# Group 0 of an embedding loop: shift and normalise moved one block on, and two weight low parts formed earlier

## The reference

```python
h = tok(x, emb0..emb3, proj0..proj3)                  # adaptive embedding: a row of one of 4 tables, times its projection
h = h + attn(layernorm(h), w1, v1, w2, conv, A, B, C, D)
h = h + ffn(layernorm(h), shared experts, 8 routed experts, top 2 by a hash of the position)
...
x1 = x @ w1_w.T + w1_b
x_conv = _silu(_depthwise_conv(x1, conv_w))           # 3 taps
x_ssm = _ssm(x_conv, A, B_ssm, C_ssm, D_ssm)          # a linear recurrence over the position
v = _silu(x @ v1_w.T + v1_b)
return x_ssm * v @ w2_w.T + w2_b
```

## Time and profile before

| | us |
|---|---|
| median of 3 runs | 439.96 (439.94 to 440.4) |
| the profiled execution, its own time | 440.18 |
| its span in the profile | 438.3 |
| PE busy | 399.5 (91%) |
| DVE, ACT, POOL busy | 272.8, 243.5, 211.5 |

### The profile page before, as it was taken

How to read it: one execution, slowest core, us unless ns; L and a number is a source line. 1 busy time by engine, 2 the same in 40 slices (tenths; PEclk the granted TensorE clock), 3 DMA queues, 4 the chain that set the end, 5 groups by cost and what they waited for, 6 DMA issues and landing times.

```text
span 438.3 us, 8454 instructions
## 1 busy us (share of the span) xinstructions
PE 399.5 (91%) x2880; PEld 351.6 (80%) x2880; DVE 272.8 (62%) x607; ACT 243.5 (56%) x435; POOL 211.5 (48%) x236
## 2 busy tenths in 40 slices
PE   3869999899998874999999999999999999998996
PEld 2858788788677863788898988988988888897885
DVE  6667998889756778464565565564554654655333
ACT  4567777768887436635535635635635536435442
POOL 6578988831005555648337247247247336433000
PEclk9999999999999989899999999999999999999999
DMA  2424111249699982101111211201301301100101
GB/s 63 145 80 161 49 58 57 65 129 323 182 312 303 239 314 96 50 0 49 53 45 48 59 40 49 84 11 48 96 0 49 96 0 49 48 0 0 49 0 48
DMA packets 32779, 38.86 MB, mean 89 GB/s; under 512 B 3461, under 2 KB 29027, under 8 KB 32624
## 3 DMA queue, kind: packets, MB, share of 16 engines
q1 hardware_dynamic: 29616, 32.99, 24.3%
q0 software_dynamic: 3136, 5.52, 4.1%
HBM read 34.56 MB, written 8.65 MB: 99 GB/s over the span
## 4 chain that ended last, share of the span: by engine, by line
PE 65%; DVE 15%; POOL 6%; ACT 6%; issue 4%; DMA 3%; DVEq 0%; SPq 0%; ACTq 0%; POOLq 0%
PE ps L1152 20%; PE ps L1153 20%; PE ps L1154 20%; DVE hid_lo L1085 3%; DMA h_in<-h_rows_dram 2%; DVE stat L963 2%; POOL bias_e L657 1%; POOL bias_e L658 1%; PE ps L1160 1%; PE ps L1271 1%; PE ps L1190 1%; DVE x_mid L1016 1%; DVE act_out L1079 1%; ACT act_out L857 1%; DVE catT_lo L956 1%
## 5 line engine op out<-in xcount | busy, mean ns | idle before, releaser
L1085 DVE SCALAR_TENSOR_TENSOR hid_lo<-act_out,hid_hi 128x512 fp32r<-128x512 f32 x64 | 54.4, 851 | 57.6 <-ACT hid_hi L870 57.6
L857 ACT ACTIVATE act_out<-ps,vec 128x512 f32<-128x512 f32 x32 | 22.0, 689 | 90.5 <-PE ps L1154 90.5
L1079 DVE SCALAR_TENSOR_TENSOR act_out<-ps,vec,act_out 128x512 f32<-128x512 f32 x32 | 24.0, 751 | 55.6 <-ACT act_out L857 55.6
L687 POOL TENSOR_TENSOR h_sb<-h_sb,bias_e 128x256 f32<-128x256 f32 x32 | 24.5, 769 | 53.6 <-DVE h2n L976 53.6
L1154 PE MATMUL ps<-h2nT_hi,sw_lo 128*128 128x512 f32 x128 | 50.0, 391 | 0.0
L1153 PE MATMUL ps<-h2nT_lo,sw_hi 128*128 128x512 f32 x128 | 50.0, 391 | 0.0
L1152 PE MATMUL ps<-h2nT_hi,sw_hi 128*128 128x512 f32 x128 | 49.9, 390 | 0.0
L680 POOL TENSOR_TENSOR zc_lo<-v_sb,zc_hi 128x256 fp32r<-128x256 f32 x32 | 28.9, 907 | 34.4 <-ACT zc_hi L847 34.4
L861 ACT ACTIVATE act_out<-ps,vec 128x512 f32<-128x512 f32 x32 | 22.1, 689 | 40.4 <-PE ps L1154 40.3
L537 POOL DMA_INDIRECT cat<-table_dram,x_ids x32 | 35.7, 1115 | 8.4 <-issue 5.8
L870 ACT ACTIVATE hid_hi<-act_out 128x512 fp32r<-128x512 f32 x64 | 39.7, 622 | 0.0
(11 more groups left out here) (133 smaller groups left out, 1254.2 us busy)
## 6 DMA issues: line engine op xcount, KB each, us to landing
toep_l<-kernel_rows_dram SPq DMA_DIRECT2D x14, 512.0 KB, 9.0
toep_r<-kernel_rows_dram SPq DMA_DIRECT2D x12, 512.0 KB, 6.4
h_rows_dram<-h_ring SPq DMA_DIRECT2D x32, 128.0 KB, 1.8
h_in<-h_rows_dram SPq DMA_DIRECT2D x8, 512.0 KB, 4.5
stage<-w_e_dram POOLq DMA_DIRECT2D x7, 512.0 KB, 3.6
out_dram<-o_sb SPq DMA_DIRECT2D x7, 512.0 KB, 3.2
bias_e<-rows_dram SPq DMA_DIRECT2D x1, 1024.0 KB, 7.3
toep_r<-kernel_rows_dram SPq DMA_DIRECT2D x4, 256.0 KB, 7.7
```

What stands on the lines that cost most here:

```text
L687: nc.gpsimd.tensor_tensor(at, at, bias_e[:, bass.ds(e, 1), :].rearrange("p o c -> p (o c)"), ALU.add).then_inc(h2_biased, 1)
L857: nc.scalar.activation(act_out[:, n % 4, :], ps[bank][:, :], ACT.Silu, bias=vec[:, C_SB1 + j:C_SB1 + j + 1]).then_inc(act_done, 1)
L1079: nc.vector.scalar_tensor_tensor(act_out[:, n % 4, :], ps[bank + 1][:, :], vec[:, C_SB3 + j:C_SB3 + j + 1], act_out[:, n % 4, :], ALU.add, ...
L1085: nc.vector.scalar_tensor_tensor(hid_lo[:, n % 4, :], act_out[:, n % 4, :], 0.5 if kind == SHARED else 0.25, f32(hid_hi[:, n % 4, :]), ALU ...
```

## The change

In group 0 the `norm` tasks of a pair of tiles no longer stand at the end of the odd block that made the pair's `rstd` usable (blocks 3, 5, 7 and block 1 of group 1), behind `aggr`. They stand in the next even block (4, 6, and 0 and 2 of group 1), right behind `cat` and ahead of `emb`. ACT's rounding of the weights, `wv_hi`, hung on the norm of tile 5 and hangs on that of tile 3. The two `wv_part`s of POOL move from the start of group 1 to the ends of blocks 6 and 7 of group 0, each behind that block's gather. Groups 1 to 3 keep their order, and nothing is added or removed.

```diff
@@ phase_a
         for r in range(RES):
             add("cat", 0, r)
             behind("out", r, 1)
-            back, pair = (0, r - 3) if r >= 3 else (1, RES - 2)
-            first_group = isinstance(i, int) and i == back
-
-            def add_norm():
-                if r % 2:
+            if r % 2 == 0:
+                back, pair = (0, r - 4) if r >= 4 else (1, r + 4)
+                if isinstance(i, int) and i == back:
                     add("norm", back, pair)
                     add("norm", back, pair + 1)
-
-            if not first_group:
-                add_norm()
+            else:
+                back, pair = (0, r - 3) if r >= 3 else (1, RES - 2)
+                if not (isinstance(i, int) and i == back):
+                    add("norm", back, pair)
+                    add("norm", back, pair + 1)
             add("emb", 0, r - 1) if r else add("emb", 1, RES - 1)
             add("stats", 0, r - 1) if r else add("stats", 1, RES - 1)
             add("aggr", 0, r - 1) if r else add("aggr", 1, RES - 1)
-            if first_group:
-                add_norm()
@@ group, POOL
             for r in range(RES):
-                if i == 1 and r == 0:
-                    wv_part(0)
-                    wv_part(1)
...
                 elif i + 1 < GROUPS:
                     gather(i + 1, r + LEAD - RES)
+                if i == 0 and r >= RES - 2:
+                    wv_part(r - RES + 2)
@@ norm, ACT
-            if r == 5:
+            if r == 3:
                 act.wait_ge(wa_in, 32)
                 nc.scalar.copy(wv_hi[:, :, :, :].rearrange("p a k n -> p (a k n)"), raw_a[:, KC * D:]).then_inc(wa_hi, 1)
```

## The result

The changed kernel takes 442.89 us (median of 6 runs, 441.98 to 444.06) beside 439.95 for the kernel before (6 runs, 439.21 to 440.4) on the same chip: ratio 1.0067, interval 1.0052 to 1.0082, +2.9 us. The forecast of 440.2 was too low, and the range, which ended at 441.3, did not hold the time. What happened is the first rival in kind and in sign ("POOL gets the memory first"), but larger than it was priced.

The account below looks back on a forecast made before the run. Bound: group 0's loop of dependences between engines, passed one for one to the end. First projection 0.1 earlier, POOL 0.6 late, the middle +0.25 taken: 439.96 + 0.25 = 440.2 us; range 439.3 to 441.3.

Parts of the forecast that it names:

- the first rival: Shifts of tiles 4, 5 wait 1.26 for POOL's `wv_lo`; first projection about 1.1 later, 441.2; chance 0.16.
- Common jitter cancels: Shift against `wv_lo`: DVE and POOL count from the same `eps`, so the 0.1 margin should survive jitter.
- the rest of the forecast: Group 0 without the lost port: the first projection, at 36.55 before, starts 0.1 earlier.
- `eps` of tiles 8, 9: Before the first projection: waits for the first half of L564 (0.66) instead of the second, 0.1 gained.
- The rival's second wait: If POOL goes first, `eps` of tiles 6, 7 also falls into the second half of `wv_lo`.
- the period: Group 0's loop: waiting for `catT_lo` costs 0.47, 0.22 comes back; net +0.25 per pair, 4.95 instead of 4.7.
- `emb` of the even tile 0.24 behind its transpose: Group 0: `catT_lo` of the even tile is ready early, so `emb` no longer waits for it; 0.22 comes back.
- `wv_hi` one pair earlier: ACT, behind `hn` of tiles 2, 3: next pair's transpose 1.5 late, but `emb` of tile 8 only 0.36 later.
- `eps` of tiles 6, 7 through before the second half: DVE's `eps` at 30.24 ends 0.1 to 0.3 before POOL's second half of `wv_lo`, so the 0.9 stall goes.
- Afterwards all engines carry the same offset: Behind the `eps` at 41.91, the offset of +0.25 should reach the end of the program on all engines.
- POOL's lag: POOL reaches L564 0.55 to 0.6 late; rival: it passes whole to every later `eps`, +0.6, 440.55, chance 0.12.
- a sign that the later stages do not pass the offset on: Sign of being wrong: an offset that changes by more than 0.5 between 45 us and the end.

Follow-up runs that it names:

- e8: The change itself measured a second time, in another series: 443.28 us, ratio 1.0045 to the kernel before.
- e5: The kernel before with its own order of shift and normalise; only `wv_hi` and the halves of `wv_lo` moved as in the change: 442.90 us, ratio 1.0043.
- e11: e6 with the second half of `wv_lo` behind block 6's gather instead of block 7's: 440.15 us, ratio 0.9999.
- e1: The change with a POOL memset of 0.33 us added ahead of the first half of `wv_lo`: 442.78 us, ratio 1.0066.
- e3: The change with both `wv_part`s back at the start of group 1, `wv_hi` left early: 440.33 us, ratio 1.0016.
- e6: The kernel before with `wv_hi` ahead of the normalisation of tile 2 and the `wv_lo` halves behind the gathers of blocks 5 and 7: 439.02 us, ratio 0.9949.
- e9: The change with POOL made to wait for the sixth shift before the first half of `wv_lo`: 441.08 us, ratio 1.0027.
- e10: e5 with POOL made to wait for the sixth shift before the first half of `wv_lo`: 440.30 us, ratio 1.0003.
- e12: e6 measured once more, beside e11: 437.68 us, ratio 0.9934.
- e7: The change's order of normalisation, with `wv_hi` and the `wv_lo` halves in the places of e6: 440.09 us, ratio 0.9979.
- e2: The change with each half of `wv_lo` written as two POOL instructions of 256 columns: 440.30 us, ratio 1.0002.
- e4: The kernel before with only shift and normalise moved as in the change, `wv_hi` and `wv_lo` as before: 440.43 us, ratio 1.0002.

## Why the prediction was wrong, step by step

**The step that failed** is in the first rival: "The two shifts of tiles 4 and 5 stand at 27.83 and 27.88, POOL's first half of `wv_lo` at 28.0: a margin of 0.1 ... The point from which it decides is that 0.1 us." The distance was forecast well (0.18 was measured, 27.09 to 27.27). The criterion was wrong. With a ready half of `wv_lo` behind a running gather the shift is held though it starts 0.18, 0.19, 0.40, 0.42 or 0.44 ahead (the change, e8, e5, e11, e1), each time 0.69 to 0.92 into the gather; with a gather or a waiting instruction behind it, it takes 0.20 to 0.22 (before, e3, e6, e9, e10, e12). By the forecast's own sums the gather stood at 26.87 and the shift at 27.83, 0.96 into it. A shift there was held in every run that had this order with halves of 512 columns, so the rival was far likelier than the 0.16 that I gave it; I took recorded starts for a race. "Common jitter cancels" was true of the distance and did not matter.

**The term that was mis-sized** is the rival's price, 1.1 at the first projection. Measured was 2.53. Followed along the path, against the forecast's times less 0.56:

- the rest of the forecast, as it stood: -0.1; the shift of tiles 4 and 5 was reached at 27.09 instead of 27.27: -0.2;
- the two shifts: 1.55 instead of 0.20, +1.35. The rival had 1.26 for it;
- the lower clock: tile 9's transpose to `emb` of tile 8 takes 0.48 (30.25 to 30.73) instead of 0.24, and `emb` to `h_ring` 2.31 (30.73 to 33.04) instead of the 1.37 of the earlier trace rows: together +1.2. No term of the forecast held this. A wait on DVE was priced at its own length, and not at what the hole that it makes in PE can bring with it;
- the shifts of tiles 6 and 7: 0.60 instead of 0.20 beside POOL's L562, +0.40, and 0.1 more ahead of them. L562 was expected at 35.15 (34.6 in this execution's count) and came at 34.54; that the *shift* would stand there, and not `eps` of tiles 8, 9, followed from everything being late;
- `eps` of tiles 8 and 9 met no L562 (0.17 at 37.38), where the forecast had left 0.2 of the 0.3 that they waited before: -0.2.

Their sum is 2.55. The rival's second wait, `eps` of tiles 6 and 7 in the second half of `wv_lo`, came to only 0.15 (0.32 instead of 0.17).

Three sums of the forecast are off by a little and decide nothing: the statistics were set 0.57 behind `h_ring`, where the list above them has 0.51; L564 follows from its own terms at 35.26, not 35.15; and 1.1 on 439.96 is 441.1, not 441.2.

**Right were:**

- the period: +0.25 per pair forecast, 4.99 instead of 4.69, and 0.25 per period in e7 beside e6;
- `emb` of the even tile 0.24 behind its transpose: 0.25 (18.49 to 18.74);
- `wv_hi` one pair earlier: the period of the pair behind it was forecast at 5.52 (23.61 to 29.13) and is 5.43 in e3 and 5.42 in e9, where the shift isn't held; and `emb` of tile 8 then follows its transpose after 0.25 (e3, 28.62 to 28.87) without the 0.92 of idle of before.

**Right in the outcome, for another reason:**

- "`eps` of tiles 6, 7 through before the second half": it took 0.32, and the stall of 1.08 was gone. But it was late by the held shift and met the second half's end. Where the shift isn't held (e9) it takes 1.76. With the shift free, the forecast's path would have failed at this next step;
- `eps` of tiles 8, 9: a wait for the first half of L564 was forecast, with none as the better bound; there was none, because it came late.

"Afterwards all engines carry the same offset" held up to 136 us: plain times of the profiled executions differ by 1.97 at the first projection and by about 1.8 from 53 to 136 us.

**POOL's lag**, a rival with 0.12 and the +0.25 of the forecast, could not be seen: the offset only shrinks a little behind 45 us.

From 140 to 190 us the offset grows by another 0.9 to about 2.7, which is the difference of the two spans. There, stretches at the lower clock lie elsewhere in each execution (before 158.0 to 161.4 and 175.1 to 178.5; after 153.1 to 156.5 and 177.0 to 183.9), and they do so in every kernel of the study. The 0.9 is more than the 0.5 which the prediction named as a sign that the later stages do not pass the offset on. I take that part for chance in the profiled execution and not for the change's: over the same stretch the two executions of one kernel, e6 and e12, gain 1.7 and 0.5 on the one of before, and those of the change 0.9 and (e8) 1.5. The medians differ by 2.94 in one series and 2.20 in the other, around the 2.53 of group 0. That all of it is chance isn't shown, since no run here has the clock alone changed.

**Left open:** why pieces of 256 columns let DVE in (e2's first shift and its `eps`; `eps` of e4 at 35.49, 0.15 ahead of L562 behind a gather, took 0.17; the first shift of tiles 6 and 7 in e5, at 33.74 ahead of L564, was held only to the gather's end, 0.47; and so was DVE's `hn` of 128x256 at 37.20 in the kernel before, in the gather of 36.95 with L564 behind it, 0.93 instead of 0.40); why a hole of about 2.2 was followed by the lower clock four times (the change, e1, e5, e8) and not in e11, and one of 1.08 once of several times (e4); whether the pair is really taken during the gather; and 1 us between the medians of e11 and e12.

## What to carry to other kernels

When a short DVE instruction on the critical path falls near POOL work, ask what POOL has *ready next* in its list, and not which recorded start is earlier. Here a ready elementwise instruction of 512 columns behind a gather held DVE off through its whole length whenever DVE came late in that gather (0.62 to 0.95 into it, seven of seven); at the gather's start it didn't, and another gather or a wait in its place never did. Put such a POOL instruction where POOL idles while DVE is busy with something that nobody waits for, or cut it small; the first turned a ratio of 1.0067 into 0.9949 and 0.9934, with the old order of the normalisation (0.9979 with the new one), the second into 1.0002, while a bare wait for the shift only passed the hold on to the next DVE instruction. And price a hold by the hole that it makes in TensorE too: here the slow clock behind the hole cost 1.2 on top of 1.35.

## What the runs showed of the hardware

- A DVE instruction with two operands in SBUF (`shift`, 0.13 to 0.15 alone) that starts 0.69 to 0.92 into a POOL gather takes 1.49 to 1.74 when a `tensor_tensor` of POOL on 128x512 stands ready behind the gather (in e1 behind a short memset), up to that instruction's end; it takes 0.20 to 0.22 for two of them where another gather or a waiting instruction stands there. Held were five executions (the change, e1, e5, e8, e11), not held six (before, e3, e6, e9, e10, e12).
- At the start of such a gather it isn't held: 0.26 for two at 27.11 in e7, 1.04 ahead of `wv_lo`.
- Ahead of pieces of 128x256 it varies: 0.19 and 0.84 for the two shifts of e2, 0.47 for the first shift of tiles 6 and 7 in e5.
- A `tensor_scalar` of DVE on 128x2 (`eps`, 0.17 alone) is held in the same way ahead of 128x512: 1.76 in e9, 1.44 in e10. Ahead of 128x256 it took 0.22 in e2 and 0.17 in e4.
- Between two POOL instructions back to back DVE was let in in e4 (0.32) and in the change (the shift at 34.66), and was not in e3 (1.71 through both).
- The held time is recorded as the DVE instruction's duration, with no idle time and no wait.
- Holes of 2.18 to 2.44 in PE's work went with 3.4 us of granted clock 0.50 in four executions of five, from 0.3 before to 0.5 behind the hole's end. Shorter ones in this loop, up to the 1.59 ahead of 36.37 in e1, did not, but for the 1.08 of e4.
